# A graph network on one core: a tile's division inside the next tile's first turn, and the running maximum in SBUF

## The chip, the cores and the metric

One core of a Trainium2 chip runs the whole program. The metric is the device time of one execution in microseconds (us). The engines are named as the profile names them: PE is TensorE, DVE is VectorE, ACT is ScalarE, POOL is GpSimd, SP is SyncE.

## What is computed

The reference is a small graph network on 3125 nodes with 16 features each and 103,125 edges sorted by their target node. Its first part is three graph convolutions with a residual and a layer norm. Its second part, which the change touches, is an edge-conditioned attention: every edge gets two 16x16 matrices out of its 16 attributes (one for the attention, one for the message), both multiplied row by row with the source node's features, and for every target node and each of the 256 positions a softmax over the node's edges weights the messages:

```python
w_m = (efeat @ W_msg + b_msg).reshape(E, in_f, -1)
w_a = (efeat @ W_attn + b_attn).reshape(E, in_f, -1)
e1, e2 = w_m * h_src, w_a * h_src              # h_src = feat[src][:, :, None]
seg_max = segment_max(e2, dst)
ex = exp(e2 - seg_max[dst])
attn = ex / segment_sum(ex, dst)[dst]
ft = segment_sum(e1 * attn, dst).sum(axis=1)    # then residual and layer norm
```

## The kernel before, in words

The first 940 us or so count edges, sort the nodes by degree and compute the three convolutions. The change leaves them alone. What follows is the stage in question.

**Tiles and units.** The sorted nodes are cut into 25 tiles of 128 nodes, one node to a partition. A tile is worked off in *units* of 8 edge slots: a unit takes the next 8 edges of each of the 128 nodes. A tile has as many units as its largest degree needs, so the count is a value that the program reads at run time (`levels`). With this data the 25 tiles have 8, 6, 6, ten times 5, ten times 4 and twice 3 units, 116 in all. Every engine runs through the same sequence of units; PE, ACT, POOL and SP don't know of tiles at all and count units in fours (`quads`), only DVE has two nested loops, tiles (L1473) and units (L1475). A softmax is kept online: a running maximum per node and position, and a running sum (denominator and numerator side by side, 2 x 256 values a node) that is faded by exp(old maximum - new maximum) whenever a unit is added.

**One turn of the loop**, in DVE's order (L1475 to L1493), with unit u finished and later units prepared:

- `weighted` (L1424): after ACT's exponentials of unit u, two products of 1024 values, message x weight, in place in `eo` (L1430).
- `rest_one` (L1369): one subtraction for unit u+4 (L1373).
- `peaks` (L1398) for unit u+1: the maximum over the 8 slots in three halvings (L1407, L1410, L1412), with a drain of DVE's pipeline behind each; then max(old, new) is formed **twice** by the loop at L1414, once into `top2` in SBUF and once into the PSUM tensor `bank[0]`, which holds the running maximum (two halves that take turns); a drain; the difference old - new for the fading (L1418), which reads `bank[0]` and the copy in `top2`; and the subtraction of the maximum from all 2048 attention values (L1421), with `eo` in SBUF and the maximum from `bank[0]` in PSUM.
- `rest_two` (L1377): one more subtraction for unit u+4 (L1380).
- `scaled` (L1385) for unit u+3: three products of 1024 values, matrix product in PSUM times the gathered neighbour features `nbr` (L1392). The slots 6 and 7 are scaled by ACT (`last_pair`, L979).
- `accumulate` (L1432): the sum of unit u out of PSUM, faded, into `acc` (L1437); PE adds unit u+1 onto it (`sums`, L791: `acc` by L797, the slots by L801, in two halves).

**At a tile's end** DVE runs `finish` (L1442) behind the last `accumulate`: a reciprocal of the 256 denominators in PSUM (L1445), a drain, the quotient (L1447), the next tile's number of units read into a register (L1449), a drain, a reduction into one column block of `ft_p` (L1451), a drain. The first unit of a tile forgets the old maximum by adding -3e38 from `pen` instead of 0.

**The queues around it.** POOL (L604 to L618) issues for each unit one indirect DMA for the edge attributes (L611) and eight for the neighbours' features (L617), each of 128 rows, with the row numbers read from `rec` in SBUF. The features of unit k may be fetched once ACT's `last_pair` of unit k-4 is done (L615), which happens in turn k-6; DVE wants them in turn k-3, ACT in turn k-2. There are four buffers for them (`SETS`), and four of `eo` (`RING`). SP loads the records of unit k+2 once the features of unit k have landed (L466 to L476).

Of the kernel before, what the change touches and what calls it, by code (L numbers as in the profile page):

```python
# [6 lines left out]
P = 128  # L7
# [5 lines left out]
ALU = mybir.AluOpType  # L13
# [5 lines left out]
E = 103125  # L19
FEAT = 16  # L20
# [9 lines left out]
SETS = 4  # L30
# [29 lines left out]
def gnn_kernel(nc, x, src, dst, edge_attr, W1, b1, W2, b2, W3, b3, W_msg, b_msg, W_attn, b_attn, out):  # L60
# [9 lines left out]
    with ExitStack() as ctx:  # L70
        def sb(name, shape, dt=F32, stack=ctx):
            return stack.enter_context(nc.sbuf_tensor(name, shape, dt))
# [155 lines left out]
        mdiff = sb("mdiff", [P, CH])  # L228
        acc = sb("acc", [P, 2 * CH])
# [3 lines left out]
        ft_p = sb("ft_p", [P, NT, FEAT])  # L233
# [253 lines left out]
        def _(pool):  # L487
# [134 lines left out]
            for t in range(NT):  # L622
                pool.indirect_dma_start(ft_nat, bass.IndirectOffsetOnAxis(ap=ids[:, t:t + 1], axis=0),
                                        ft_p[:, t, :], None).then_inc(s_out, 16)
# [396 lines left out]
        def _(dve):  # L1021
# [340 lines left out]
            dve.memset(bank[0][:], 0.0)  # L1362
            dve.memset(acc[:], 0.0)
            dve.memset(pen[:, 0:1], -3e38)
# [33 lines left out]
            def peaks(ring, first, old, new, seen):  # L1398

                def wide(v):  # L1400
                    return v.rearrange("p (c o) -> p c o", o=FEAT)

                before = bank[0][:, bass.ds(old * CH, CH)]
                after = bank[0][:, bass.ds(new * CH, CH)]
# [3 lines left out]
                                  ).then_inc(s_attr_free, 1)  # L1408
                dve.drain()  # L1409
                dve.tensor_tensor(top2[:], top4[:, 0:2 * CH], top4[:, 2 * CH:4 * CH], ALU.max)  # L1410
                dve.drain()
                dve.tensor_tensor(top1[:], top2[:, 0:CH], top2[:, CH:2 * CH], ALU.max)  # L1412
                dve.drain()
                for copy in (top2[:, 0:CH], after):  # L1414
                    dve.scalar_tensor_tensor(out=copy, in0=before, scalar=pen[:, bass.ds(first, 1)], in1=top1[:],
                                             op0=ALU.add, op1=ALU.max)
                dve.drain()  # L1417
                dve.scalar_tensor_tensor(out=mdiff[:], in0=before, scalar=pen[:, bass.ds(first, 1)], in1=top2[:, 0:CH],  # L1418
# [23 lines left out]
            def finish(tile, units, unit):  # L1442

                parts = pair[:, bass.ds(unit, 1), :].rearrange("p r (c m o) -> p (r c) m o", m=2, o=FEAT)
                dve.reciprocal(rden[:].rearrange("p (c o) -> p c o", o=FEAT), parts[:, :, 0, :])  # L1445
                dve.drain()
                dve.tensor_tensor(ratio[:].rearrange("p (c o) -> p c o", o=FEAT), parts[:, :, 1, :],  # L1447
                                  rden[:].rearrange("p (c o) -> p c o", o=FEAT), ALU.mult)
                dve.reg_mov(units, dve.value_load(levels[0:1, bass.ds(tile + 1, 1)], min_val=1, max_val=E))  # L1449
                dve.drain()  # L1450
                dve.tensor_reduce(ft_p[:, bass.ds(tile, 1), :].rearrange("p a f -> p (a f)"),  # L1451
                                  ratio[:].rearrange("p (i o) -> p o i", o=FEAT), AX_X, ALU.add)
                dve.drain()
# [18 lines left out]
            dve.reg_mov(units, dve.value_load(levels[0:1, 0:1], min_val=1, max_val=E))  # L1472
            with dve.Fori(0, NT) as t:  # L1473
                n = dve.snap(units, min_val=1, max_val=E)
                with dve.Fori(0, n) as level:  # L1475
                    u = dve.snap(step, min_val=0, max_val=MANY)
                    even = dve.snap(u % 2, min_val=0, max_val=1)
                    odd = dve.snap((u + 1) % 2, min_val=0, max_val=1)
                    held = dve.snap(u % SETS, min_val=0, max_val=SETS - 1)
                    later = dve.snap((u + 3) % SETS, min_val=0, max_val=SETS - 1)  # L1480
                    here = dve.snap(u % RING, min_val=0, max_val=RING - 1)
                    following = dve.snap((u + 1) % RING, min_val=0, max_val=RING - 1)
                    fourth = dve.snap((u + 3) % RING, min_val=0, max_val=RING - 1)
# [51 lines left out]
```

## Time and profile before

| what | us |
|---|---|
| median of 3 runs | 2688.94 |
| lowest and highest | 2686.95, 2690.07 |
| the profiled execution | 2685.97 |
| its span in the trace | 2684.2 |
| DVE busy in the span | 2113.0 (79%) |
| PE busy | 2030.2 (76%) |
| ACT busy | 1413.4 (53%) |
| POOL busy | 1288.1 (48%) |

The span runs from the first to the last recorded instruction; the profiled execution's time is 1.8 us longer, for what lies around it. Shares over the whole span mix the early stages with the loop that the change is in, so the loop has to be read by itself. "PEclk" is TensorE's granted clock as a share of full speed. A duration on DVE includes the filling and emptying of its pipeline, so that the next instruction can start before the one in front has its end: the distance between two starts is the price of an instruction, and the duration is not.

### The profile page before, as it was taken

What the parts mean: (1) busy time and instruction counts of PE and PEld (TensorE: products, weight loads), DVE (VectorE), ACT (ScalarE), POOL (GpSimd) and SP (SyncE); (2) the same over time, 40 slices, a digit from 0 to 9 for tenths busy, and PEclk for the clock granted to TensorE, in tenths of its full rate; (3) what the DMA queues carried; (4) which work ended last, traced back from release to release, by engine and by line L of the source; (5) the groups of instructions that cost most, each with busy time, mean ns of one, the idle gap of its engine ahead of it and who ended that gap; (6) DMA issues with size and microseconds to landing.
All of it is one profiled execution on the core that took longest, in us unless ns stands there. A gap on an engine that the chain in (4) does not pass through costs nothing.

```text
span 2684.2 us, 39375 instructions
## 1 busy us (share of the span) xinstructions
PE 2030.2 (76%) x5872; PEld 714.5 (27%) x5873; DVE 2113.0 (79%) x4340; ACT 1413.4 (53%) x4967; POOL 1288.1 (48%) x1556
## 2 busy tenths in 40 slices
PE   3766777777699648887888888888888788888782
PEld 1111111111333313333333333333333333333330
DVE  5876888887401149999999999999999889999883
ACT  5123333321001047777767777777776666766762
POOL 2100000012455477666666666666666665666653
PEclk9655555555898859999999999999999999999996
DMA  2000000000000011110000000101000000100110
GB/s 32 14 0 26 0 0 0 0 0 1 20 11 11 16 13 11 10 10 10 10 9 10 10 10 9 10 10 10 9 10 10 10 9 10 9 10 10 10 7 9
DMA packets 87256, 26.29 MB, mean 10 GB/s; under 512 B 63117, under 2 KB 84223, under 8 KB 87103
## 3 DMA queue, kind: packets, MB, share of 16 engines
q0 software_dynamic: 37824, 18.62, 6.4%
q1 hardware_dynamic: 49327, 6.96, 1.7%
q10 hardware_dynamic: 80, 0.43, 0.1%
q8 instruction: 10, 0.16, 0.0%
q14 instruction: 15, 0.12, 0.0%
HBM read 23.30 MB, written 2.51 MB: 10 GB/s over the span
## 4 chain that ended last, share of the span: by engine, by line
issue 28%; DVE 26%; PE 17%; DVEq 15%; POOL 5%; POOLq 4%; ACT 3%; DMA 1%; ACTq 0%; PEldq 0%; SPq 0%; PEld 0%
PE pair L801 10%; DVE eo L1392 7%; DVEq L1409 3%; DVE top L1407 3%; ACT eo L988 3%; PE bank L658 3%; DVE hot L1132 3%; DVE hot L1130 3%; PE pair L658 2%; DVE top L1410 2%; DVE eo L1430 2%; DVEq L1417 2%; DVE rden L1445 2%; DVEq L1153 2%; PE pw L788 1%
## 5 line engine op out<-in xcount | busy, mean ns | idle before, releaser
L617 POOL DMA_INDIRECT nbr<-table,rec x960 | 963.7, 1004 | 463.1 <-issue 258.2
L801 PE MATMUL pair<-eo,ident 128*128 128x512 f32 x1856 | 903.0, 632 | 123.0 <-DVE eo L1430 120.1
L988 ACT ACTIVATE eo<-pw,nbr 128x32 f32<-128x32 f32 x3776 | 686.9, 407 | 0.0
L801 PEld LDWEIGHTS pair<-eo,ident 128*128 128x128 f32 x1856 | 364.8, 202 | 603.1 <-issue 586.9
L1392 DVE TENSOR_TENSOR eo<-pw,nbr 128x1024 f32 (+1 forms) x357 | 417.0, 1218 | 43.4 <-PE pw L788 42.9
L1130 DVE TENSOR_SCALAR hot<-iota_key,near_key 128x500 bf16<-128x500 f16 x974 | 341.0, 350 | 119.3 <-issue 55.5
L788 PE MATMUL pw<-wk,termsT 100*128 100x512 bf16 x954 | 288.5, 384 | 128.6 <-issue 64.6
L977 ACT ACTIVATE eo<-eo 128x2048 f32<-128x2048 f32 x117 | 223.5, 1910 | 206.1 <-DVE eo L1421 206.1
L658 PE MATMUL bank<-hot 128*128 128x500 bf16 x488 | 230.3, 603 | 127.2 <-DVE hot L1132 103.5
L1430 DVE TENSOR_TENSOR eo<-eo x232 | 273.5, 1221 | 30.9 <-issue 27.1
L658 PE MATMUL pair<-hot 128*128 128x500 bf16 x486 | 228.5, 602 | 51.6 <-DVE hot L1132 45.4
L1421 DVE TENSOR_TENSOR eo<-eo,bank (+1 forms) x117 | 266.4, 2277 | 0.0
L1132 DVE TENSOR_SCALAR hot<-iota_low,near_low 128x128 bf16<-128x128 bf16 x974 | 246.3, 253 | 0.0
L966 ACT CAST termsT<-pt 100x512 bf16<-100x512 f32 x240 | 139.3, 581 | 100.9 <-PE pt L770 100.9
L544 POOL TENSOR_SCALAR place<-place 128x25 f32<-128x25 f32 x1 | 0.3, 253 | 384.3 <-ACTq L927 384.3
L770 PE MATMUL pt<-identb,terms 128*100 128x128 bf16 x960 | 95.9, 223 | 116.0 <-ACT termsT L966 87.7
L611 POOL DMA_INDIRECT attr<-in_edge_attr_dram,rec x120 | 115.6, 964 | 136.5 <-DMA rec<-unit_recs 98.4
L869 ACT CAST counts<-pair 128x500 f32 x79 | 45.5, 576 | 225.2 <-PEq L676 225.2
L869 ACT CAST counts<-bank 128x500 f32 x79 | 45.5, 576 | 197.8 <-PEq L676 195.5
L788 PEld LDWEIGHTS pw<-wk,termsT 100*128 100x128 bf16 x954 | 68.1, 97 | 286.7 <-issue 286.4
L1407 DVE TENSOR_TENSOR top<-eo 128x1024 f32 (+1 forms) x117 | 142.7, 1220 | 0.0
L770 PEld LDWEIGHTS pt<-identb,terms 128*100 128x100 bf16 x960 | 78.0, 127 | 235.6 <-issue 235.6
(237 smaller groups left out, 1834.7 us busy)
## 6 DMA issues: line engine op xcount, KB each, us to landing
nbr<-table,rec POOLq DMA_INDIRECT x960, 2.4
rec<-unit_recs SPq DMA_DIRECT2D x122, 8.0 KB, 1.7
attr<-in_edge_attr_dram,rec POOLq DMA_INDIRECT x120, 2.5
unit_recs<-place SPq DMA_DIRECT2D x27, 64.0 KB, 1.6
shared<-key_row SPq DMA_DIRECT2D x1, 1600.0 KB, 6.7
counts<-in_dst_dram SPq DMA_DIRECT2D x1, 448.0 KB
counts<-in_src_dram SPq DMA_DIRECT2D x1, 448.0 KB
place<-in_src_dram,at_i POOLq DMA_INDIRECT x26, 2.6
```

What stands on the lines that cost most here:

```text
L617: pool.indirect_dma_start(nbr[:, b, j * FEAT:(j + 1) * FEAT], None, table, bass.IndirectOffsetOnAxis(ap=rec[:, b, j:j + 1], axis=0)).then_ ...
L658: return pe.matmul(bank[v][:, 0:NG * WIN], hot_low[:, k, :], hot_key[:, k, :], start=first, stop=False, skip_group_check=True)
L788: mm = pe.matmul(pw[:, 2 * (k % 2) + j, :], termsT[:, unit, lo:lo + P], wk[:], start=True, stop=True)
L801: mm = pe.matmul(total, ident[:], eo[:, ring, j * 2 * CH:(j + 1) * 2 * CH], start=False, stop=(j == SLOT - 1), skip_group_check=True)
L977: act.activation(here, here, ACT.Exp).then_inc(s_ex, 1)
L988: done = act.activation(eo[:, ring, lo:lo + wide], pw[:, j - 4, c * wide:(c + 1) * wide], ACT.Copy, scale=nbr[:, held, j * FEAT + c:j * FE ...
L1130: dve.tensor_scalar(hot_key[:, slot, :].rearrange("p (a d) -> p a d", a=NG), iota_key[:], near_key[v][:, k], None, ALU.is_equal)
L1132: return dve.tensor_scalar(hot_low[:, slot, :], iota_low[:], near_low[v][:, k], None, ALU.is_equal)
L1392: dve.tensor_tensor(eo[:, bass.ds(ring, 1), k * 4 * CH:(k + 1) * 4 * CH] .rearrange("p r (c f) -> p (r c) f", f=2 * FEAT), pw[:, 2 * (k % ...
L1407: dve.tensor_tensor(wide(top4[:]), attention(ring, 0, 4), attention(ring, 4, 8), ALU.max).then_inc(s_attr_free, 1)
L1421: dve.tensor_tensor(here, here, wide(after).unsqueeze(1).broadcast_to([P, SLOT, FEAT, FEAT]), ALU.subtract).then_inc(s_d, 1)
L1430: dve.tensor_tensor(here, here, attention(ring, 4 * half, 4 * half + 4), ALU.mult).then_inc(s_p, 1)
```

## The change

A finished tile is no longer divided out behind its last unit. The first unit of every tile is taken out of the unit loop (`one_unit` with a tile number), and in its `peaks` the three steps of the division of the tile before stand ahead of the three drains that are there already: the reciprocal behind L1407, the quotient behind L1410, the reduction behind L1412. The next tile's number of units is read behind `weighted` in that unit. In the very first tile the division works on a bank of ones, and its result goes into an extra column block of `ft_p`; the last tile is divided behind the loop. The running maximum is kept in a new SBUF tensor `peak` and formed once: the second copy is gone, and L1418 and L1421 read the maximum from SBUF. The counts of the other engines' instructions are as before.

```diff
--- before.py
+++ after.py
@@ -226,11 +226,12 @@
         top2 = sb("top2", [P, 2 * CH])
         top1 = sb("top1", [P, CH])
         mdiff = sb("mdiff", [P, CH])
+        peak = sb("peak", [P, 2 * CH])
         acc = sb("acc", [P, 2 * CH])
         fade = sb("fade", [P, CH])
         rden = sb("rden", [P, CH])
         ratio = sb("ratio", [P, CH])
-        ft_p = sb("ft_p", [P, NT, FEAT])
+        ft_p = sb("ft_p", [P, NT + 1, FEAT])
         x2 = sb("x2", [P, NG, FEAT])
         x2_sq = sb("x2_sq", [P, NG, FEAT])
 
@@ -621,7 +622,7 @@
             pool.wait_ge(s_ft, 1)
             for t in range(NT):
                 pool.indirect_dma_start(ft_nat, bass.IndirectOffsetOnAxis(ap=ids[:, t:t + 1], axis=0),
-                                        ft_p[:, t, :], None).then_inc(s_out, 16)
+                                        ft_p[:, t + 1, :], None).then_inc(s_out, 16)
             pool.wait_ge(s_out, 16 * NT)
 
         @block.tensor
@@ -1359,8 +1360,9 @@
             dve.drain().then_inc(s_x1, 1)
 
             dve.memset(terms[:, :, :, TERMS * FEAT:KROWS], 1.0)
-            dve.memset(bank[0][:], 0.0)
+            dve.memset(peak[:], 0.0)
             dve.memset(acc[:], 0.0)
+            dve.memset(pair[:, 1, :], 1.0)
             dve.memset(pen[:, 0:1], -3e38)
             dve.memset(pen[:, 1:2], 0.0)
             dve.drain().then_inc(s_stage, 1)
@@ -1395,27 +1397,32 @@
                                       h_src.unsqueeze(2).broadcast_to([P, 2 * FEAT, 2 * FEAT]),
                                       ALU.mult).then_inc((s_pair0_free, s_pair1_dve, s_scaled)[k], 1)
 
-            def peaks(ring, first, old, new, seen):
+            def peaks(ring, first, old, new, seen, ended=None):
 
                 def wide(v):
                     return v.rearrange("p (c o) -> p c o", o=FEAT)
 
-                before = bank[0][:, bass.ds(old * CH, CH)]
-                after = bank[0][:, bass.ds(new * CH, CH)]
+                before = peak[:, bass.ds(old * CH, CH)]
+                after = peak[:, bass.ds(new * CH, CH)]
                 dve.wait_ge(s_pair1_act, seen + SETS + 1)
                 dve.sem_inc(s_settled_dve, 1)
                 dve.tensor_tensor(wide(top4[:]), attention(ring, 0, 4), attention(ring, 4, 8), ALU.max
                                   ).then_inc(s_attr_free, 1)
+                if ended:
+                    inverse(*ended)
                 dve.drain()
                 dve.tensor_tensor(top2[:], top4[:, 0:2 * CH], top4[:, 2 * CH:4 * CH], ALU.max)
+                if ended:
+                    quotient(*ended)
                 dve.drain()
                 dve.tensor_tensor(top1[:], top2[:, 0:CH], top2[:, CH:2 * CH], ALU.max)
-                dve.drain()
-                for copy in (top2[:, 0:CH], after):
-                    dve.scalar_tensor_tensor(out=copy, in0=before, scalar=pen[:, bass.ds(first, 1)], in1=top1[:],
-                                             op0=ALU.add, op1=ALU.max)
-                dve.drain()
-                dve.scalar_tensor_tensor(out=mdiff[:], in0=before, scalar=pen[:, bass.ds(first, 1)], in1=top2[:, 0:CH],
+                if ended:
+                    outcome(*ended)
+                dve.drain()
+                dve.scalar_tensor_tensor(out=after, in0=before, scalar=pen[:, bass.ds(first, 1)], in1=top1[:],
+                                         op0=ALU.add, op1=ALU.max)
+                dve.drain()
+                dve.scalar_tensor_tensor(out=mdiff[:], in0=before, scalar=pen[:, bass.ds(first, 1)], in1=after,
                                          op0=ALU.add, op1=ALU.subtract).then_inc(s_md, 1)
                 here = attention(ring).rearrange("p (s c) o -> p s c o", s=SLOT)
                 dve.tensor_tensor(here, here, wide(after).unsqueeze(1).broadcast_to([P, SLOT, FEAT, FEAT]),
@@ -1439,18 +1446,23 @@
                                   fade[:].rearrange("p (c o) -> p c o", o=FEAT)
                                   .unsqueeze(2).broadcast_to([P, FEAT, 2, FEAT]), ALU.mult).then_inc(s_accd, 1)
 
-            def finish(tile, units, unit):
-
-                parts = pair[:, bass.ds(unit, 1), :].rearrange("p r (c m o) -> p (r c) m o", m=2, o=FEAT)
-                dve.reciprocal(rden[:].rearrange("p (c o) -> p c o", o=FEAT), parts[:, :, 0, :])
-                dve.drain()
-                dve.tensor_tensor(ratio[:].rearrange("p (c o) -> p c o", o=FEAT), parts[:, :, 1, :],
+            def ended_sums(unit):
+
+                return pair[:, bass.ds(unit, 1), :].rearrange("p r (c m o) -> p (r c) m o", m=2, o=FEAT)
+
+            def inverse(tile, unit):
+
+                dve.reciprocal(rden[:].rearrange("p (c o) -> p c o", o=FEAT), ended_sums(unit)[:, :, 0, :])
+
+            def quotient(tile, unit):
+
+                dve.tensor_tensor(ratio[:].rearrange("p (c o) -> p c o", o=FEAT), ended_sums(unit)[:, :, 1, :],
                                   rden[:].rearrange("p (c o) -> p c o", o=FEAT), ALU.mult)
-                dve.reg_mov(units, dve.value_load(levels[0:1, bass.ds(tile + 1, 1)], min_val=1, max_val=E))
-                dve.drain()
+
+            def outcome(tile, unit):
+
                 dve.tensor_reduce(ft_p[:, bass.ds(tile, 1), :].rearrange("p a f -> p (a f)"),
                                   ratio[:].rearrange("p (i o) -> p o i", o=FEAT), AX_X, ALU.add)
-                dve.drain()
 
             for u in range(2):
                 rest_one(u, u, u)
@@ -1470,30 +1482,44 @@
             dve.reg_mov(step, 0)
             units = dve.alloc_register("dve_units")
             dve.reg_mov(units, dve.value_load(levels[0:1, 0:1], min_val=1, max_val=E))
+            coming = dve.alloc_register("dve_coming")
+
+            def one_unit(remaining, tile):
+
+                u = dve.snap(step, min_val=0, max_val=MANY)
+                even = dve.snap(u % 2, min_val=0, max_val=1)
+                odd = dve.snap((u + 1) % 2, min_val=0, max_val=1)
+                held = dve.snap(u % SETS, min_val=0, max_val=SETS - 1)
+                later = dve.snap((u + 3) % SETS, min_val=0, max_val=SETS - 1)
+                here = dve.snap(u % RING, min_val=0, max_val=RING - 1)
+                following = dve.snap((u + 1) % RING, min_val=0, max_val=RING - 1)
+                fourth = dve.snap((u + 3) % RING, min_val=0, max_val=RING - 1)
+                remaining()
+                dve.reg_alu(left, left, 2, ALU.min)
+                within = dve.snap(dve.snap(left, min_val=1, max_val=2) - 1, min_val=0, max_val=1)
+                weighted(here, u)
+                if tile is not None:
+                    dve.reg_mov(coming, dve.value_load(levels[0:1, bass.ds(tile + 1, 1)], min_val=1, max_val=E))
+                rest_one(even, held, u + LEAD)
+                peaks(following, within, even, odd, u + 1, None if tile is None else (tile, odd))
+                rest_two(even, u + LEAD)
+                scaled(fourth, later, u + 3)
+                dve.reg_add(step, step, 1)
+                accumulate(even, u)
+
             with dve.Fori(0, NT) as t:
                 n = dve.snap(units, min_val=1, max_val=E)
-                with dve.Fori(0, n) as level:
-                    u = dve.snap(step, min_val=0, max_val=MANY)
-                    even = dve.snap(u % 2, min_val=0, max_val=1)
-                    odd = dve.snap((u + 1) % 2, min_val=0, max_val=1)
-                    held = dve.snap(u % SETS, min_val=0, max_val=SETS - 1)
-                    later = dve.snap((u + 3) % SETS, min_val=0, max_val=SETS - 1)
-                    here = dve.snap(u % RING, min_val=0, max_val=RING - 1)
-                    following = dve.snap((u + 1) % RING, min_val=0, max_val=RING - 1)
-                    fourth = dve.snap((u + 3) % RING, min_val=0, max_val=RING - 1)
-                    dve.reg_sub(left, n, level)
-                    dve.reg_alu(left, left, 2, ALU.min)
-                    within = dve.snap(dve.snap(left, min_val=1, max_val=2) - 1, min_val=0, max_val=1)
-                    weighted(here, u)
-                    rest_one(even, held, u + LEAD)
-                    peaks(following, within, even, odd, u + 1)
-                    rest_two(even, u + LEAD)
-                    scaled(fourth, later, u + 3)
-                    dve.reg_add(step, step, 1)
-                    accumulate(even, u)
-                ended = dve.snap(step, min_val=1, max_val=MANY)
-                last = dve.snap((ended + 1) % 2, min_val=0, max_val=1)
-                finish(t, units, last)
+                one_unit(lambda: dve.reg_add(left, n, 0), t)
+                with dve.Fori(1, n) as level:
+                    one_unit(lambda: dve.reg_sub(left, n, level), None)
+                dve.reg_add(units, coming, 0)
+            total = dve.snap(step, min_val=1, max_val=MANY)
+            last = dve.snap((total + 1) % 2, min_val=0, max_val=1)
+            inverse(NT, last)
+            dve.drain()
+            quotient(NT, last)
+            dve.drain()
+            outcome(NT, last)
             dve.sem_inc(s_scaled, SETS)
             dve.drain().then_inc(s_ft, 1)
 
```

## Rows read from the trace of the kernel before

**Rows 1.** the page: span

```profile
span 2684.2 us, 39375 instructions
```

**Rows 2.** DVE instruction groups, 1075 to 2650 us: busy, mean ns | idle before

```profile
L1392 DVE TENSOR_TENSOR eo<-pw,nbr 128x1024 f32 x330 | 385.2, 1218 | 22.2 <-PE pw L788 22.1
L1430 DVE TENSOR_TENSOR eo<-eo x220 | 259.4, 1221 | 27.1 <-issue 27.1
```

**Rows 3.** timeline of DVE, 2002 to 2033 us: start, us, instruction [idle]

```profile
2002.28 0.48 DVE L1415 SCALAR_TENSOR_TENSOR top<-bank,pen,top 128x256 f32<-128x256 f32 x1 [0.20 <-issue]
2002.68 0.48 DVE L1415 SCALAR_TENSOR_TENSOR bank<-bank,pen,top 128x256 f32 x1
...
2003.64 2.28 DVE L1421 TENSOR_TENSOR eo<-eo,bank  x1
...
2010.03 2.35 DVE L1430 TENSOR_TENSOR eo<-eo  x2
2012.30 0.29 DVE L1373 TENSOR_TENSOR res<-attr,terms 128x128 f32 x1
2012.50 1.22 DVE L1407 TENSOR_TENSOR top<-eo 128x1024 f32 x1
2013.81 0.69 DVE L1410 TENSOR_TENSOR top<-top 128x512 f32<-128x512 f32 x1
...
2015.21 0.49 DVE L1415 SCALAR_TENSOR_TENSOR top<-bank,pen,top 128x256 f32<-128x256 f32 x1 [0.20 <-issue]
...
2022.96 1.75 DVE L1445 RECIPROCAL rden<-pair 128x256 f32 x1
2024.89 0.42 DVE L1447 TENSOR_TENSOR ratio<-pair,rden 128x256 f32<-128x256 f32 x1 [0.18 <-issue]
2025.88 0.58 DVE L1451 TENSOR_REDUCE ft_p<-ratio 128x256 f32 x1 [0.56 <-issue]
2027.59 2.36 DVE L1430 TENSOR_TENSOR eo<-eo  x2 [1.13 <-issue]
...
2032.77 0.48 DVE L1415 SCALAR_TENSOR_TENSOR top<-bank,pen,top 128x256 f32<-128x256 f32 x1 [0.20 <-issue]
```

**Rows 4.** timeline of PE, 2015 to 2035 us, same columns

```profile
2015.99 0.59 PE L788 MATMUL pw<-wk,termsT 100*128 100x512 bf16 x2 [0.93 <-issue]
...
2028.96 5.88 PE L801 MATMUL pair<-eo,ident 128*128 128x512 f32 x8 [4.67 <-DVE eo L1430]
```

**Rows 5.** timeline of ACT, 2010 to 2021 us, same columns

```profile
2010.07 5.82 ACT L988 ACTIVATE eo<-pw,nbr 128x32 f32<-128x32 f32 x32
...
2018.97 1.91 ACT L977 ACTIVATE eo<-eo 128x2048 f32<-128x2048 f32 x1 [1.78 <-DVE eo L1421]
```

**Rows 6.** windows: us, PE, PEld, DVE, ACT, POOL busy, PEclk, DMA share, GB/s

```profile
2022.00:2024.00 2.00, 1.73 (x6) 0.42 (x4) 2.00 (x3) 1.99 (x9) 1.56 (x2) 1.00 0.17 12
...
2029.00:2033.00 4.00, 4.00 (x5) 1.78 (x6) 3.63 (x6) 0.41 (x1) 2.77 (x3) 0.50 0.05 4
```

**Rows 7.** timeline of POOL, 2003 to 2013 us, same columns

```profile
2003.91 0.94 POOL L617 DMA_INDIRECT nbr<-table,rec  x1 [2.19 <-ACT eo L988]
...
2010.15 1.91 POOL L617 DMA_INDIRECT nbr<-table,rec  x1 [0.30 <-issue]
2012.37 1.03 POOL L617 DMA_INDIRECT nbr<-table,rec  x1 [0.30 <-issue]
```

**Rows 8.** all neighbour gathers: busy, mean ns; then ns min/median/max

```profile
L617 POOL DMA_INDIRECT nbr<-table,rec x960 | 963.7, 1004 | 463.1 <-issue 258.2
L617 POOL DMA_INDIRECT nbr<-table,rec x960: 938/944/2018, 936.8 to 2604.5; - x192
```

**Rows 9.** chain of waits: DVE sequencer (DVEq) and L1430 behind an accumulate

```profile
1952.42 0.20 DVEq L1475
...
1953.55 0.20 DVE eo L1430
```

**Rows 10.** the page: a DMA queue that loads instructions (packets, MB, share)

```profile
q8 instruction: 10, 0.16, 0.0%
```

## Prediction

> **What bounds the kernel now.** I read the DVE groups first, then a timeline of one plain turn and one with a tile's end, engine by engine, then POOL's rows. The span is 2684.2 us [rows 1]. In the loop DVE is the bound: from L1415 to L1415 a plain turn takes 2015.21 - 2002.28 = 12.93 us, and DVE has no gap in it but the drains [rows 3]. Other engines wait in it: ACT 1.78 us for L1421 [rows 5], PE 0.93 us ahead of a product [rows 4], POOL up to 2.19 us for ACT [rows 7]. A turn with a tile's end takes 2032.77 - 2015.21 = 17.56 us, 4.63 more [rows 3]. Of the 25 ends the last lies behind the last unit. The kernel has 116 units: L1430 runs twice a turn, 220 times in this window, and the rest of its runs lie outside [rows 2]. Behind a tile's end DVE also waits for PE at L1392, 22.2 us in all [rows 2]: PE idled 4.67 us, and its next eight matmuls took 5.88 us [rows 4], because the granted clock fell from 1.00 to 0.50, from the 2.4 GHz level to 1.2 [rows 6].
>
> **A. The second copy of the maximum goes.** It occupies 2002.68 - 2002.28 = 0.40 us of DVE in every turn [rows 3]: 115 x 0.40 = **-46 us**. That three instructions read SBUF in place of PSUM I cost at nothing on DVE: L1392 with a PSUM input has a mean of 1218 ns, L1430 of the same size with two SBUF inputs 1221 ns [rows 2]. The 0.20 us of idle before L1415 [rows 3] is the drain and address work; with one output less it could lose up to 0.1 (-12 us), or nothing; I take nothing, since the drain is still there.
> Does another engine take over at 12.53? ACT's `last_pair` takes 5.82 us [rows 5]; behind it come on PE one product, four slots' sums and a transpose, and two copies on ACT before the next `last_pair`. From L1421's end (2005.92) ACT needed until 2015.89, the end of its 5.82 us from 2010.07; PE went on at 2015.99 [rows 3 to 5]. Taking PE's piece as 4.3 us and ACT's copies as 2.2 us, estimates from the distances in this timeline, that loop closes in about 12.45 us. It is just under 12.53, so A is real but about the last that can be had this way.
>
> **B. The division moves.** What a tile's end costs now is instructions and gaps: before L1447 0.18, before L1451 0.56, before the next L1430 1.13 us [rows 3], 1.87 together. Put ahead of drains that exist, each step adds its duration less the overlap of about 0.08 between two undrained instructions: 1.75 - 0.08, 0.42 - 0.08 and 0.58 - 0.08, together 2.51 [rows 3]. Saved: 4.63 - 2.51 = 2.12, 24 times: **-51 us**. The last tile's division costs the same as before. Queued behind the three steps are L1418, for which ACT's fading waits, and L1421, for which its exponentials wait, and behind these PE's transpose, L1392 and `accumulate`: all come 2.5 us later in that turn, when no one else is the bound.
>
> **C. PE's idle time shrinks.** PE now has the weighted values on time and works through both half sums before it waits about 2.5 us, in place of 4.67 at once. No row shows what the clock does behind 2.5 us. Bounds: all 22.2 us of DVE's waits go, or all stay; I take **-20 us**, since of the turn's long matmuls only those behind the wait could be slow, and PE has 0.93 us to spare there [rows 4].
>
> **D. The new loop edges.** The first unit stands alone, so DVE's sequencer has two edges a tile (outer loop to first unit, first unit to inner loop) and a register read behind `weighted`. It now runs ahead: at 1952.42 it is at the loop's head while L1430 starts at 1953.55 [rows 9]. A tile's end lost 1.13 us with the pipeline drained [rows 3], so an edge costs between 0 and 1.1; I take 0.25 for each edge, nearer to the row with the lead, as both edges have a full `accumulate` as cover: 24 x 0.5 = **+12 us**, between 0 and 53. The one memset more costs under 1 us. The output DMAs are the same 25.
>
> **E. What SBUF reads do to POOL.** This is the price that the diff doesn't show. A gather normally takes 944 ns, with 0.30 idle before it, so POOL issues one per 1.25 us [rows 7, 8]. One that starts at 2010.15, 0.12 us into L1430, takes 1.91 us [rows 3, 7]: it is held until the first of the two products is through. One that starts at 2012.37 while L1373 runs takes 1.03. But one at 2003.91, inside the 2.28 us of L1421, takes 0.94 [rows 3, 7]. So far L1421 has an input in PSUM, L1430 and L1373 have both in SBUF. The holds already are 960 x (1004 - 944) ns = 58 us [rows 8], half a microsecond a unit, and cost nothing. With `peak` in SBUF, L1421 becomes the longest instruction with two SBUF inputs.
> Walk through a turn of 12.53, counted from L1430, with each gather either at once or held to the end of the instruction. L1421 lies at 6.14 to 8.30. A gather held there is let go at 8.30; the next start at 9.55, 10.79, 12.04, then 0.76 in the next turn, held to 1.10 by L1430, 2.35, held to 2.43 by L1373, 3.67, 4.92, and 6.17, held to 8.30. That is **eight in a turn where a unit needs nine** (one for the attributes, eight for the features), with 0.34 + 0.08 + 2.13 = 2.55 us of holds. A tile of five units then asks of POOL 45 x 1.247 = 56.1 plus 4 x 2.55 and about 1.3 in the divided turn, 67.6 us, where DVE asks for 5 x 12.53 + 2.51 = 65.2. Short: 2.4 us; by the same sum 1.2 for four units, nothing for three, 3.6 for six, 6.2 for eight; over the tiles 8, 6, 6, ten of 5, ten of 4, two of 3: 50 us. POOL starts with a lead: the features may be fetched in turn k-6 and are wanted in k-3, three turns (38 us) less about 12 for the eight gathers and some for landing; I take 18 us of usable lead. So **+32 us**; bounds 0 (holds fall into other phases, D's edges give POOL time) and 65 (no lead, worse phases).
> The page "SBUF — State Buffer" of the Trainium skill, section "Who interferes with whom", infers that a two-input DVE instruction holds only the read side and so does not stall descriptor generation; by that E would be 0 and the time 2581. The 1.91 us row speaks against it, since these gathers read their row numbers from SBUF.
>
> **The sum.** Against the profiled execution, 2685.97: -46 -51 -20 +12 +32 = -73, so 2613. The median of the runs shown is 3 us above it; I give **2614**. A measurement of this kernel can tell about 0.2% (5 us) from no change.
>
> **Rivals.**
> 1. *POOL never becomes the bound* (E = 0): 2613 - 32 = 2581, with small edges 2570. For it: POOL has 2 us to spare in a turn now [rows 7]. Against it: the walk gives eight, not nine. Chance 0.25.
> 2. *PE's clock still falls at each tile and the edges are dear*: C = 0 and D = 30: 2613 + 20 + 18 = 2651. For it: 0.50 behind 4.67 us [rows 6]. Against it: partly the same time as E, since POOL catches up while DVE waits. Chance 0.16.
> 3. *Slower: POOL sets the pace throughout.* Place: the nine gathers. If holds came to over 2.9 us a unit, POOL would need 9 x 1.247 + 2.9 = 14.1 us, and 116 of these are 1640, what the loop takes now (115 turns of 12.93, 24 ends of 4.63 and 22 us of waits, 1620, plus the last unit). With 3.4 (0.95 as at L1430, 2.13 at L1421, 0.3 at L1407) it is 14.6 a unit: 1696 less the lead, 2725. For it: both long holds can fall in one turn. Against it: they do so in the walk, with only 2.55. Chance 0.05.
> 4. *Instruction fetch.* DVE's loop body doubles. The page shows 10 loads of instructions on a queue [rows 10], far fewer than the 116 turns; a load's price is in no row. Were DVE to wait at both edges of a tile for as long as the slowest gather takes, 2.02 us [rows 8], 24 x 4.04 = 97 us would give 2613 + 97 = 2710; it decides from 73 / 24 = 3 us a tile. A rule of the Trainium skill's "Runtime: NRT & Kernel Launch", section "Instruction fetch mechanics", says that a branch out of the two pages in reach stalls. Chance 0.03.
> 5. *Nothing much moves*, as DVE was held by PE's loop all along: 2685. Against it: DVE's gapless turns. Chance 0.01.
>
> **How the numbers follow.** The forecast has 0.50. Range: from rival 1 with its small edges, 2566, to rival 2, 2652; it leaves out the slower cases and some of the tails. Faster 0.91, same 0.02, slower 0.07.
>
> **What would show it.** A plain turn of 12.53 on DVE; no idle of 1.13 before L1430; a turn with a division at 15.0 to 15.6. On POOL, gathers of up to 3.1 us (0.94 + 2.13) that start early in L1421, a mean near 1.2 us, and fewer waits for ACT. On DVE, waits of about 1.2 us at L1392 in the second half of the stage, put down to PE or a DMA, where POOL was late. Wrong would be: gathers in L1421 at 0.94 (then rival 1), PEclk of 0.50 in every tile (rival 2), or plain turns over 12.6.

## The result, and where the time went

The changed kernel takes 2592.56 us (median of 4 runs, 2590.3 to 2594.34) beside 2688.01 for the kernel before: a ratio of 0.9644, 95% interval 0.9627 to 0.966. The profiled execution took 2591.05 us with a span of 2589.2. The forecast was 2614, the range 2566 to 2652. So the direction and the order of size were right, and 21 us more were gained than the sum had. The terms tell more than the total: of the five, only the division's was near; two came to about 60% of what the sum had, and two to nothing.

From the page of the changed kernel, its first line and sections 1 and 5:

```profile
span 2589.2 us, 39091 instructions
...
PE 2000.3 (77%) x5872; PEld 710.1 (27%) x5873; DVE 2061.6 (80%) x4227; ACT 1410.8 (54%) x4967; POOL 1419.5 (55%) x1556
...
L618 POOL DMA_INDIRECT nbr<-table,rec x960 | 1085.9, 1131 | 337.9 <-issue 282.6
...
L1437 DVE TENSOR_TENSOR eo<-eo x232 | 272.5, 1216 | 3.7 <-ACT eo L978 3.7
```

POOL is busier although it issues what it did before: a gather's mean went from 1004 ns [rows 8] to 1131. DVE's idle time before L1437 (L1430 before) was 27.1 us in the loop [rows 2] and is 3.7 in the whole run, all of it one wait at the start.

The timeline of DVE in the changed kernel, a divided turn's end and one plain turn (start, us, instruction, idle before it); L1422 answers to L1415, L1437 to L1430, L1428 to L1421:

```profile
1982.22 0.48 DVE L1422 SCALAR_TENSOR_TENSOR peak<-peak,pen,top 128x256 f32 x1 [0.30 <-issue]
...
1989.60 2.34 DVE L1437 TENSOR_TENSOR eo<-eo  x2
1991.87 0.28 DVE L1375 TENSOR_TENSOR res<-attr,terms 128x128 f32 x1
1992.07 1.21 DVE L1409 TENSOR_TENSOR top<-eo 128x1024 f32 x1
1993.37 0.69 DVE L1414 TENSOR_TENSOR top<-top 128x512 f32<-128x512 f32 x1
1994.14 0.43 DVE L1418 TENSOR_TENSOR top<-top 128x256 f32<-128x256 f32 x1
1994.92 0.49 DVE L1422 SCALAR_TENSOR_TENSOR peak<-peak,pen,top 128x256 f32 x1 [0.36 <-issue]
1995.49 0.48 DVE L1425 SCALAR_TENSOR_TENSOR mdiff<-peak,pen 128x256 f32 x1
1995.89 2.28 DVE L1428 TENSOR_TENSOR eo<-eo,peak  x1
```

L1422 to L1422 is 1994.92 - 1982.22 = 12.70 us. Most plain turns take 12.69, where 12.93 was [rows 3]. The copy is gone (0.40), but the idle time ahead of the maximum went from 0.20 [rows 3] to 0.36. A turn with a division takes 15.10 us, where a tile's end took 17.56. From the first L1425 of the loop (L1418 before) to the last, which is 115 turns, the sum goes from 1624.3 to 1531.6 us. Call a turn late by what it takes beyond the usual turn of its kind. The 92.7 us then split without a rest: 115 x 0.24 = 27.6 for the maximum, 24 x (4.64 - 2.41) = 53.5 for the division, and the late time, 26.0 us before and 14.4 after, 11.6. The 4.64 is 17.57 - 12.93, the 2.41 is 15.10 - 12.69. Of what is left of the 95 us between the two executions, 1.5 lie ahead of the loop and 0.8 behind it.

The late time comes from PE: 13.3 of the 14.4 us lie between the products of L1394, which take their input from PE. PE's timeline in the same divided turn, then the windows with the granted clock (us, PE, PEld, DVE, ACT, POOL busy, PEclk, DMA share, GB/s):

```profile
1985.92 0.40 PE L771 MATMUL pt<-identb,terms 128*100 128x128 bf16 x4 [1.45 <-DVE terms L1382]
1986.91 0.59 PE L789 MATMUL pw<-wk,termsT 100*128 100x512 bf16 x2 [0.60 <-issue]
1988.13 0.64 PE L771 MATMUL pt<-identb,terms 128*100 128x128 bf16 x4 [0.62 <-ACT termsT L967]
```

```profile
1984.00:1986.00 2.00, 0.55 (x4) 0.11 (x3) 2.00 (x3) 0.40 (x1) 1.70 (x2) 1.00 0.06 4
1986.00:1988.00 2.00, 0.91 (x6) 0.30 (x6) 2.00 (x3) 1.98 (x2) 1.39 (x3) 0.96 0.05 4
1988.00:1990.00 2.00, 1.87 (x8) 1.03 (x9) 2.00 (x3) 1.12 (x4) 1.70 (x2) 0.50 0.12 8
...
1992.00:1994.00 2.00, 2.00 (x6) 0.95 (x5) 1.91 (x3) 2.00 (x14) 1.70 (x2) 1.00 0.08 8
```

The idle time of 4.67 us in one piece [rows 4] has become three pieces of 1.45, 0.60 and 0.62, but the clock still falls to 0.50, the 1.2 GHz level, within the third of them and is back at 1.00 before 1992. Over these 115 turns it is at 0.50 in 24 stretches of 116 us together, beside 25 of 147 us before.

### The profile page after: what moved, and what is told of

The parts are those of the page before. It is cut to its first block, busy times and chain, and to the rows that moved or that the text cites. A ratio compares the mean times of both kernels' runs of the same rounds, so it can differ in the third digit from the quotient of the medians.

```text
span 2589.2 us, 39091 instructions
## 1 busy us (share of the span) xinstructions
PE 2000.3 (77%) x5872; PEld 710.1 (27%) x5873; DVE 2061.6 (80%) x4227; ACT 1410.8 (54%) x4967; POOL 1419.5 (55%) x1556
## 3 DMA queue, kind: packets, MB, share of 16 engines
HBM read 23.30 MB, written 2.51 MB: 10 GB/s over the span
## 4 chain that ended last, share of the span: by engine, by line
DVE 31%; issue 30%; DVEq 17%; PE 11%; POOLq 5%; POOL 5%; ACT 1%; DMA 1%; ACTq 0%; PEldq 0%; PEld 0%; SPq 0%
DVE eo L1394 8%; DVE top L1409 4%; DVEq L1413 4%; PE pair L802 3%; DVE hot L1131 3%; DVE hot L1133 3%; PE bank L659 2%; PE pair L659 2%; DVE top L1414 2%; DVE peak L1422 2%; DVE rden L1455 2%; DVEq L1154 2%; DVE eo L1437 2%; DVEq L1394 1%; DVE top L1418 1%
## 5 line engine op out<-in xcount | busy, mean ns | idle before, releaser
L618 POOL DMA_INDIRECT nbr<-table,rec x960 | 1085.9, 1131 | 337.9 <-issue 282.6
L802 PE MATMUL pair<-eo,ident 128*128 128x512 f32 x1856 | 857.0, 605 | 10.2 <-DVE eo L1437 7.6
L802 PEld LDWEIGHTS pair<-eo,ident 128*128 128x128 f32 x1856 | 353.2, 194 | 468.4 <-issue 452.2
L1394 DVE TENSOR_TENSOR eo<-pw,nbr 128x1024 f32 (+1 forms) x357 | 417.8, 1216 | 30.5 <-PE pw L789 28.2
L1131 DVE TENSOR_SCALAR hot<-iota_key,near_key 128x500 bf16<-128x500 f16 x974 | 339.9, 349 | 117.4 <-issue 53.5
L789 PE MATMUL pw<-wk,termsT 100*128 100x512 bf16 x954 | 304.5, 406 | 137.9 <-issue 77.1
L659 PE MATMUL bank<-hot 128*128 128x500 bf16 x488 | 221.6, 581 | 132.4 <-DVE hot L1133 108.6
L1437 DVE TENSOR_TENSOR eo<-eo x232 | 272.5, 1216 | 3.7 <-ACT eo L978 3.7
L1428 DVE TENSOR_TENSOR eo<-eo,peak (+1 forms) x117 | 267.3, 2285 | 0.0
L659 PE MATMUL pair<-hot 128*128 128x500 bf16 x486 | 223.0, 589 | 56.3 <-DVE hot L1133 50.6
L612 POOL DMA_INDIRECT attr<-in_edge_attr_dram,rec x120 | 125.1, 1043 | 45.3 <-issue 27.6
L798 PE MATMUL pair<-acc,ident 128*128 128x512 f32 x232 | 146.1, 716 | 1.5 <-issue 0.2
```

The source lines that it names most:

```text
L618: pool.indirect_dma_start(nbr[:, b, j * FEAT:(j + 1) * FEAT], None, table, bass.IndirectOffsetOnAxis(ap=rec[:, b, j:j + 1], axis=0)).then_ ...
L659: return pe.matmul(bank[v][:, 0:NG * WIN], hot_low[:, k, :], hot_key[:, k, :], start=first, stop=False, skip_group_check=True)
L789: mm = pe.matmul(pw[:, 2 * (k % 2) + j, :], termsT[:, unit, lo:lo + P], wk[:], start=True, stop=True)
L802: mm = pe.matmul(total, ident[:], eo[:, ring, j * 2 * CH:(j + 1) * 2 * CH], start=False, stop=(j == SLOT - 1), skip_group_check=True)
L1131: dve.tensor_scalar(hot_key[:, slot, :].rearrange("p (a d) -> p a d", a=NG), iota_key[:], near_key[v][:, k], None, ALU.is_equal)
L1394: dve.tensor_tensor(eo[:, bass.ds(ring, 1), k * 4 * CH:(k + 1) * 4 * CH] .rearrange("p r (c f) -> p (r c) f", f=2 * FEAT), pw[:, 2 * (k % ...
```

## What POOL's holds look like now

The timeline of POOL in the changed kernel, beside the DVE rows above:

```profile
1993.27 0.94 POOL L612 DMA_INDIRECT attr<-in_edge_attr_dram,rec  x1 [0.30 <-issue]
1996.49 2.50 POOL L618 DMA_INDIRECT nbr<-table,rec  x1 [2.27 <-ACT eo L989]
1999.30 0.94 POOL L618 DMA_INDIRECT nbr<-table,rec  x1 [0.30 <-issue]
```

The gather that starts at 1996.49 does so 0.60 us into L1428 (1995.89) and ends at 1998.99: it was held for 1.56 us, until 2.16 us of L1428 were over. All 115 gathers that start within L1428 end alike, 3.10 or 3.11 us behind its start. Before, a gather in the middle of that instruction took 0.94 [rows 7], and none of the 213 that start within it took over 0.96. This part of step E is as predicted, to the tenth of a microsecond. But POOL waited 2.27 us for ACT ahead of it: it still has its lead, and so none of it reaches DVE. The waits view of the changed kernel (who waited for whom, us in total, times, longest) says the same for the stage from 1100 to 2530 us:

```profile
POOL nbr L618 <- ACT eo L989: 53.2, 29, 2.3
```

## The experiments

Three series of four runs were made, each on one chip, with the kernel before beside them. The first ran on a chip on which the kernel before took 2899.18 us (2888.5 to 2913.34), 8% more than elsewhere. Its profiles show idle time within an engine's own instructions, as ACT's timeline in e_divide does:

```profile
1389.68 0.29 ACT L989 ACTIVATE eo<-pw,nbr 128x32 f32<-128x32 f32 x1 [0.43 <-issue]
1390.39 2.07 ACT L989 ACTIVATE eo<-pw,nbr 128x32 f32<-128x32 f32 x11 [0.42 <-issue]
```

Why that chip did so is not settled. All four kernels of that series were run again (labels with f_) where the kernel before took 2688.14 us (second series) and 2687.45 us (third), and the readings below rest on these. The changed kernel itself ran in neither series; its 2592.56 us stand beside 2688.01.

**The division alone** (e_divide, f_divide). The changed kernel, with the maximum as it was:

```diff
-                before = peak[:, bass.ds(old * CH, CH)]
-                after = peak[:, bass.ds(new * CH, CH)]
+                before = bank[0][:, bass.ds(old * CH, CH)]
+                after = bank[0][:, bass.ds(new * CH, CH)]
...
+                for copy in (top2[:, 0:CH], after):
```

> The changed kernel with the maximum kept as before (two copies, PSUM), so only the division moves. Theory 1 (three parts that add: the division's move 53 us, the maximum 28 us, shorter waits for PE about 12 us): plain turns of 12.93 us, divided turns of about 15.35, time about 2688 - 53 - 12 to 20 = 2615 to 2623 us. Theory 2 (POOL's holds under L1428 are what leaves the late turns of 12.9 and 13.7 us): without them the time would come within 10 us of the changed kernel's, 2592 to 2602. Gathers that start in the subtraction of the maximum should take 0.94 us again, none over 2.1 us.

> The kernel of e_divide again, because the first series ran on a chip where the kernel before took 2899 us and every engine shows idle time inside its own instruction stream. Where the kernel before takes about 2688: theory 1 (the parts add) 2615 to 2623 us, ratio 0.973 to 0.976, plain turns of 12.93; theory 2 (POOL's holds are what leaves the late turns) ratio 0.964 to 0.968.

On the first chip 2816.07 us, a ratio of 0.9703 (0.9655 to 0.975). In the second series 2616.28, ratio 0.9732 (0.9716 to 0.9748): 71.9 us, which is theory 1. Plain turns take 12.93, divided ones 15.41, so the division adds 2.48 where it added 4.64, which makes 24 x 2.16 = 52 us; the other 20 are late time (26.0 us before, 5.7 here). The gathers are at 1042 ns on average and none is over 2.01 us; those that start in the subtraction, which has its input from PSUM again, take at most 0.96.

**The maximum alone** (e_peak, f_peak). The kernel before, with `peak` in SBUF formed once:

```diff
+        peak = sb("peak", [P, 2 * CH])
...
-                for copy in (top2[:, 0:CH], after):
+                dve.scalar_tensor_tensor(out=after, in0=before, ...
```

> The kernel before with the maximum formed once and kept in SBUF; the division stays at the tile's end. Theory 1: plain turns of 12.69 us (0.40 less for the copy, 0.16 more of idle ahead of the sum), a tile's end of 17.3, and the waits for PE behind it at least as long as before (22 us): time 2688 - 28 = 2660, 2658 to 2668. Theory 2 (the extra 0.16 us comes from the peeled unit and not from the addresses): plain turns of 12.53 and 2642. Gathers of up to 3 us show here too.

> The kernel of e_peak again, for the same reason. Where the kernel before takes about 2688: theory 1 (0.24 us less a turn) 2658 to 2668, ratio 0.989 to 0.993, plain turns of 12.69; theory 2 (0.16 us comes from the peeled unit) ratio 0.983. If the chip is like the first one, the ratio is 1.01 again, and then it is the chip on which the holds cost time.

On the first chip 2925.87 us, a ratio of 1.0096 (1.0065 to 1.0128), so a little slower. Why is open: POOL still waits 278.5 us for ACT there between 1075 and 2560 us, so the holds aren't shown to be the cause. In the second series 2664.61, ratio 0.9916 (0.99 to 0.9933): 23.5 us, as theory 1 has it. Plain turns take 12.69 with the 0.36 us of idle in each, so that idle comes with `peak` and not with the peeled unit. The gathers' mean is 1122 ns. The late time is 32.0 us, 6 more than before. The two parts add up: 71.9 + 23.5 = 95.4 us, and the change brings 95.5.

**One gather less** (e_seven, f_seven). The changed kernel; the features of slot 7 are zeros:

```diff
-                    for j in range(SLOT):
+                    for j in range(SLOT - 1):
                         pool.indirect_dma_start(nbr[...]
```

> The changed kernel with seven neighbour gathers a unit in place of eight; the features of slot 7 are left out (zeros). POOL's work falls by a ninth, DVE's, PE's and ACT's stay. Theory 1 (POOL keeps its lead, its holds cost nothing): within 4 us of the changed kernel. Theory 2 (POOL is part of the late turns, as step E of the prediction had it): 8 to 14 us faster, the turns of 12.9 and 13.7 us gone.

> The kernel of e_seven again (seven neighbour gathers a unit, slot 7's features left out), on a chip where the kernel before takes about 2688. Theory 1 (at 12.69 us a turn POOL keeps its lead in the changed kernel, its 192 us of holds cost nothing): 2588 to 2595, like the changed kernel. Theory 2 (POOL is part of the late turns): 2578 to 2584.

On the first chip 2746.22 us, a ratio of 0.9456 (0.9422 to 0.9491) to the kernel before. There the changed kernel wasn't run, so this run says nothing on the gather alone. In the third series 2591.28 (2589.68 to 2592.09), which is the changed kernel's 2592.56 within the spread: POOL is not the bound. The holds per gather even grew, to a mean of 1234 ns: POOL waits for ACT in nearly every turn, and in 85 of 114 cases the gather behind that wait starts 0.1 to 0.6 us into the subtraction. It cost nothing.

**One gather more** (e_ten, f_ten), into a tensor that nobody reads:

```diff
+                    pool.indirect_dma_start(extra[:, b, :], None, table,
+                                            bass.IndirectOffsetOnAxis(ap=rec[:, b, 0:1], axis=0)
+                                            ).then_inc(s_nbr[b], 16)
```

> The changed kernel with one gather more a unit, into a tensor that nobody reads. Theory 1 (POOL works 9 x 1.25 + 1.65 of holds = 12.9 us a unit where a unit has 13.35 on average, so it is 0.45 us a unit from being the bound): with ten it needs about 14.1 us or more a unit and becomes the bound: 116 x 0.8 us or more, less its lead of some 30 us: 2592 + 60 to 2592 + 130. Theory 2 (POOL has room to spare, the holds shrink when it is loaded): under 2610.

> The kernel of e_ten again (one gather more a unit), on a chip where the kernel before takes about 2688. Theory 1 (POOL works 12.9 us a unit where the changed kernel gives it 13.35 on average): it becomes the bound with about 14.1 us a unit, 2592 + 60 to 2592 + 130. Theory 2 (POOL has room to spare): under 2610.

On the first chip 3008.95 us, a ratio of 1.0363 (1.0316 to 1.041). In the third series 2680.32, ratio 0.9968 (0.9957 to 0.9979), 88 us more than the changed kernel: a tenth instruction turns POOL into the bound and takes nearly the whole gain away. POOL no longer waits for ACT, and between 1075 and 2560 us DVE waits 84.4 us at the scaling. So POOL is within one gather a unit, 1.25 us, of being it.

**One slot's sum less on PE** (e_sum7). The changed kernel; slot 7 is left out of the sums:

```diff
-                for j in range(4 * half, 4 * half + 4):
+                for j in range(4 * half, 4 * half + 4 - half):
```

> The changed kernel; PE leaves slot 7 out of the second half sum, 0.86 us less on PE between ACT's last_pair and the next transpose, nothing less on DVE, ACT and POOL. Theory 1 (the late turns of 12.9 and 13.7 us, 14 us in all, come from the loop through PE and ACT after the clock has fallen behind a divided turn): the late turns go, 10 to 15 us faster than the changed kernel, 2578 to 2583. Theory 2 (they come from POOL): no change, 2590 to 2595.

2584.34 us (2582.21 to 2585.53), 8 less than the changed kernel. By the turns' lengths the late time falls from 14.4 to 4.5 us. So the loop through PE and ACT is the larger part of it, as theory 1 says, though 10 to 15 us were expected; the rest stays open.

**The maximum in one place** (e_copy). DVE forms the new maximum in `top2`, and ACT copies it to `peak` behind the fading, so no address of it is worked out at run time:

```diff
-                dve.scalar_tensor_tensor(out=after, in0=before, ...
+                dve.scalar_tensor_tensor(out=top2[:, 0:CH], in0=peak[:], ...
...
                 act.activation(fade[:], mdiff[:], ACT.Exp)
+                act.copy(peak[:], top2[:, 0:CH]).then_inc(s_fade, 1)
```

Ahead of the loop DVE copies the first maximum into `peak` once.

> The changed kernel, with the running maximum in one place instead of two that take turns: DVE forms the new maximum in top2 and ACT copies it to peak behind the fading, so that no address of the maximum is worked out at run time. Theory 1 (the 0.16 us of extra idle ahead of the new maximum is the address work of peak): the idle falls from 0.36 to 0.2 or less, plain turns of 12.5 us, but the loop through PE and ACT closes at about 12.5 as well, so 10 to 20 us faster: 2572 to 2583. Theory 2 (the idle is the drain or the scalar operand): turns stay 12.69, time 2590 to 2595; ACT's copy lies in its 1.78 us of waiting and costs nothing.

2635.67 us (2633.78 to 2638.34), a ratio of 0.9805 (0.9789 to 0.9822): 43 us *slower* than the changed kernel, which neither theory had, though its undisturbed turns take 12.52. DVE and POOL in its timeline, then DVE's and POOL's groups from 1075 to 2560 us (busy, mean ns | idle before, releaser):

```profile
1503.71 0.48 DVE L1421 SCALAR_TENSOR_TENSOR top<-peak,pen,top 128x256 f32<-128x256 f32 x1 [0.18 <-issue]
...
1504.67 2.28 DVE L1427 TENSOR_TENSOR eo<-eo,top 128x2048 f32 x1
1504.74 3.04 POOL L618 DMA_INDIRECT nbr<-table,rec  x1 [0.30 <-issue]
```

```profile
L1395 DVE TENSOR_TENSOR eo<-pw,nbr 128x1024 f32 x324 | 383.0, 1217 | 64.7 <-PE pw L789 63.1 <-issue 0.7
...
L618 POOL DMA_INDIRECT nbr<-table,rec x862 | 1064.7, 1235 | 262.6 <-issue 255.6 <-DMA rec<-unit_recs 4.6 <-DVE eo L1395 2.4
```

The idle ahead of the maximum is back at 0.18: the 0.16 us was address work. But a gather is now held for 2.10 us in L1427, POOL no longer waits for ACT in its gathers (no such row among them, 53.2 us in the changed kernel), and DVE waits 64.7 us at the scaling. The first feature gather of unit k, which in the changed kernel starts at most 1.6 us behind the difference of turn k-6 (once the stage has run in), starts mostly 17 to 22 us behind it here: the lead is used up. That made a third theory, the one of step E, and two runs to test it against ACT's copy.

**The same with seven gathers** (e_copy7); slot 7's features are zeros.

> The kernel of e_copy (turns of 12.52 us, 2636 us) with seven neighbour gathers a unit; slot 7's features are left out. Theory 1 (at 12.52 us a turn only eight gathers fit where nine are needed, so POOL is the bound, as the walk of the prediction has it): eight now suffice and the time falls to 2575 to 2585, 50 us less than e_copy, no waits of 3 us at the scaling. Theory 2 (e_copy is slow because ACT's copy lengthens the loop through PE and ACT): the time stays within 10 us of 2636.

2576.58 us (2575.9 to 2577.22), 59 less than e_copy. ACT's copy is still in it, so the copy isn't what made e_copy slow. In the changed kernel the same edit brought 1 us.

**The same with the subtraction in two halves** (e_split):

```diff
+                for half in range(2):
+                    here = attention(ring, 4 * half, 4 * half + 4)...
+                    done = dve.tensor_tensor(here, here, wide(top2[:, 0:CH]).unsqueeze(1)
+                                             .broadcast_to([P, SLOT // 2, FEAT, FEAT]), ALU.subtract)
+                done.then_inc(s_d, 1)
```

> The kernel of e_copy with the subtraction of the maximum cut in two instructions of 1024 values, so that no hold of a gather can last over about 1.1 us; 0.07 us a turn more on DVE. Theory 1 (the length of that one instruction makes POOL the bound): holds fall from 298 us to under 200, turns of 12.59, 2578 to 2590, 50 us less than e_copy and a little less than the changed kernel. Theory 2 (ACT's copy is the cause, or the sum of the holds stays the same because more gathers are held): 2620 to 2645.

2585.74 us (2583.64 to 2587.64), a ratio of 0.9618 (0.9602 to 0.9635), with the whole computation done: 50 us less than e_copy for one instruction *more* on DVE. Its gathers and its DVE groups from 1075 to 2520 us:

```profile
L618 POOL DMA_INDIRECT nbr<-table,rec x960: 938/947/1977, 938.3 to 2508.4; - x192
```

```profile
L1428 DVE TENSOR_TENSOR eo<-eo,top 128x1024 f32 x218 | 256.4, 1218 | 0.0
```

No gather takes over 1.98 us, the mean is 1061 ns (1229 in e_copy), and the commonest plain turns take 12.57 and 12.58. It is the fastest version with the full computation, by 7 us; its runs lie below those of the changed kernel, while the intervals of the ratios still touch.

## Why the prediction was right, and where it was not

The total came nearer than its terms, and that is luck in part: A and C brought 27 us less than reckoned, while B brought 2.5 more and D and E cost 44 less.

**A, the second copy: -46 predicted, -28 measured.** The 0.40 us went as said, and the reads from SBUF cost DVE nothing (L1428 has the 2.28 us of L1421). The step that failed is "I take nothing" for the 0.20 us of idle: I had bounded it by a gain and by nothing, and it went the other way, to 0.36. So a plain turn is 12.69, over the 12.6 that was the prediction's own sign of being wrong. The register instructions of DVE's sequencer (DVEq) show where the time goes, here in the changed kernel:

```profile
L1422 DVEq FUSED_REGOPS  x232: 57/91/133, 1000.1 to 2531.8; - x116
```

Before, one of 93 ns stood between the drain and the first copy, and the other, of 117 ns, ran behind the first copy's start, where it cost nothing. With one copy both, now 133 and 83 ns, stand between the drain and the only instruction. In e_copy, where the maximum has no run-time address, one of 65 ns is left, the idle is 0.18 and the turn 12.52 us. So the addresses of `peak` are the cause.

**B, the division: -51 predicted, -53.5 measured** in the changed kernel, 2.41 us for a division against 2.51 reckoned; 2.48 in f_divide. The steps stand ahead of drains that are paid for anyway.

**C, PE's idle time: -20 predicted, -11.6 measured.** The clock does fall in the divided turn. The late time moved and became less: before, 24.4 of the 26.0 us lay in the first plain turn behind a tile's end, and now 10.0 of the 14.4 lie in the second plain turn behind a divided one. In f_divide, where the turn is 12.93, it shrinks by 20 us, as predicted; with the turn of 12.69 it is 9 us more. The clock alone doesn't make that difference: it is at 0.50 for longer in f_divide (126 us) and in e_sum7 (201 us), which are less late (5.7 and 4.5 us). I read it as the shorter turn leaving the loop through PE and ACT less room, since e_sum7, which shortens that loop, takes 8 us away. POOL's gathers are not the cause, since f_seven, with one fewer, gains 1 us.

**D, the loop edges: +12 predicted, nothing measured.** Before L1437 there is no idle behind either edge. The sequencer's lead covers both, as the row that I weighed against 1.13 us said [rows 9]; I should have gone with it altogether.

**E, POOL: +32 predicted, nothing measured.** So rival 1 is what happened, though the holds that were to speak against it came, 960 x (1131 - 944) ns = 180 us of them against 58 before, the longest gather with 3.04 us. What failed is the length of turn that the walk was made with, 12.53 in place of 12.69. Walk again with 12.69 and L1428 at 6.30 to 8.46: starts at 8.46, 9.71, 10.95, 12.20, 0.76 held to 1.10, 2.35 held to 2.43, 3.67, 4.92, 6.17, which now lies *ahead* of L1428, and 7.42, held to 8.46. That is nine gathers in a turn, with 1.5 us of holds, in place of eight with 2.55. Nine is what a unit needs. The trace has this walk, counted from L1437 at 1495.37:

```profile
1495.37 2.35 DVE L1437 TENSOR_TENSOR eo<-eo  x2
1501.55 1.02 POOL L612 DMA_INDIRECT attr<-in_edge_attr_dram,rec  x1 [0.30 <-ACT eo L989]
1501.66 2.29 DVE L1428 TENSOR_TENSOR eo<-eo,peak  x1
1502.87 1.89 POOL L618 DMA_INDIRECT nbr<-table,rec  x1 [0.30 <-issue]
```

The gather at 6.18 is 0.11 us ahead of L1428, and the next, at 7.50, is held for 0.95 us. Apart from the loop's end, all 47 turns of at most 12.85 us in which POOL waits for nobody for longer than that 0.30 have nine starts, with 1.55 us of holds on average. e_copy, whose turn is 12.52, is the case that the prediction walked through. There the gather at 6.17 starts 0.07 us inside L1427 (1504.74 and 1504.67), and all 43 such turns have eight starts, with 2.64 us of holds; the neighbour gathers alone have 960 x (1229 - 944) ns = 274 us, and the lead is gone. A turn shorter by 0.17 us came with a kernel 43 us slower. The bound of 0 for E had to carry the case, and A's error was what hid it: two terms that I took as independent were not.

The page "SBUF — State Buffer" of the Trainium skill, section "Who interferes with whom", infers that such DVE instructions do not stall descriptor generation. By the gather of 1996.49 such an instruction does hold a GpSimd indirect DMA, for the rest of its 2.16 us; for these gathers the measurement decides. The section's other sentence, that they contend with a GpSimd instruction that reads SBUF, agrees with it, since the gathers read their row numbers from SBUF. Whether it is that reading or the descriptor generation that waits, no run here shows.

**The other rivals.** The clock still falls (rival 2), but the late time is 14 us and not the 26 of before, and the edges cost nothing. POOL is the bound throughout (rival 3) in e_copy and f_ten, not here. Instruction fetch (rival 4) doesn't show: the page of the profile still has 10 loads on the queue of [rows 10], and there is no idle at the loop's edges.

**Left open.** A maximum in PSUM, copied to SBUF by ACT, should keep L1428 free of holds at one copy, as in f_divide, but DVE and ACT would then read one PSUM bank at the same time; it wasn't tried. What made the first chip slower is open too.

## What to carry to other kernels

Put work ahead of drains that are paid for anyway: here it cost its instructions and no gaps. When an instruction of VectorE gets its second input from SBUF instead of PSUM, look at what GpSimd issues meanwhile: count the indirect DMAs that fit in a turn, do it again for a turn that is 0.2 us longer and one that is shorter, and cut the longest such instruction in two if the count falls short. With that bound so near, a saving on the bounding engine can cost time, and terms of a sum that share the turn's length must be worked out together.

## What the runs showed of the hardware that I had not expected

The hold is strict and ends a little ahead of the DVE instruction's recorded end: a gather that starts t us into the subtraction of 2048 values with two SBUF inputs (2.28 us) is lengthened by 2.16 - t (t = 0.60: 1.56; t = 0.07 in e_copy: 2.10). Whether a gather starts 0.11 us ahead of that instruction or 0.07 us inside it decides between nine and eight gathers in a turn. And the granted clock fell to 0.50 within the last of three pauses of PE, of 1.45, 0.60 and 0.62 us, with short matmuls between them.
